# Attention with the values stationary: output by column, sums by a product with ones, reciprocals on ScalarE

## What is computed

```python
q = (xq @ Wq.T).reshape(B, SQ, NUM_HEADS, HEAD_DIM)      # B 8, SQ 256, 16 heads of 16
kv = (xkv @ Wkv.T).reshape(B, SKV, 2, NUM_HEADS, HEAD_DIM)  # SKV 77
att = jax.nn.softmax(jnp.einsum('bxhd,byhd->bhxy', q, k) * scale, axis=-1)
x = jnp.einsum('bhxy,byhd->bxhd', att, v).reshape(B, SQ, H)
return x @ Wout.T + bout
```

## Time and profile before

| | |
|---|---|
| median of 3 runs | 866.01 us (864.85 to 867.98) |
| profiled execution, its own time | 865.35 us |
| its span | 863.6 us, so 1.75 us lie outside of it |
| attention of layer 0, about | 6 to 145 us of the span |
| attention of layer 1, about | 242 to 381 us |

### The profile page before, as it was taken

How to read it: one execution, slowest core, us unless ns; L and a number is a source line. 1 busy time by engine, 2 the same in 40 slices (tenths; PEclk the granted TensorE clock), 3 DMA queues, 4 the chain that set the end, 5 groups by cost and what they waited for, 6 DMA issues and landing times.

```text
span 863.6 us, 17182 instructions
## 1 busy us (share of the span) xinstructions
PE 835.3 (97%) x5664; PEld 766.5 (89%) x5664; DVE 539.7 (62%) x1132; ACT 427.2 (49%) x938; POOL 276.7 (32%) x329
## 2 busy tenths in 40 slices
PE   8899999999979999999999999999999999999997
PEld 6788988999958989878887999999899999989986
DVE  4777764556687888465446574736456473645558
ACT  3666665777765666532323553616254361615331
POOL 5243414877773452145550001020200102020140
PEclk9999999999999999999999999999999999999999
DMA  5423237877520000201113432314233232413262
GB/s 209 116 69 128 66 117 286 260 219 224 175 77 8 7 6 6 87 17 44 60 44 90 133 90 70 106 41 134 60 97 95 80 89 61 128 39 100 64 194 99
DMA packets 74853, 86.26 MB, mean 100 GB/s; under 512 B 31418, under 2 KB 47484, under 8 KB 74678
## 3 DMA queue, kind: packets, MB, share of 16 engines
q1 hardware_dynamic: 67590, 69.65, 27.0%
q10 hardware_dynamic: 3664, 9.46, 3.1%
q0 software_dynamic: 3552, 6.55, 2.3%
HBM read 63.32 MB, written 23.63 MB: 101 GB/s over the span
## 4 chain that ended last, share of the span: by engine, by line
PE 83%; SPq 5%; DVE 4%; DMA 2%; ACT 2%; issue 2%; POOL 2%; DVEq 0%; ACTq 0%; POOLq 0%
PE score L292 13%; PE score L293 13%; PE score L294 13%; PE bank_p L298 11%; PE bank L603 7%; PE bank_p L299 6%; SPq L371 5%; PE bank_p L594 3%; PE bank L615 3%; PE bank L623 2%; PE bank L544 2%; PE score L583 2%; DMA v_blk<-values 1%; DVE residual L1911 1%; PE bank L957 1%
## 5 line engine op out<-in xcount | busy, mean ns | idle before, releaser
L1257 ACT ACTIVATE silu<-score 128x366 f32<-128x366 f32 (+1 forms) x144 | 72.6, 504 | 274.0 <-PE score L294 274.0
L298 PE MATMUL bank_p<-w_both,hid_hi 128*122 128x512 f32 (+1 forms) x432 | 152.5, 396 | 0.5 <-DVE hid_lo L1653 0.5
L1645 DVE TENSOR_TENSOR prod<-silu,score 128x366 f32<-128x366 f32 (+1 forms) x144 | 82.2, 571 | 110.6 <-ACT silu L1257 109.6
L292 PE MATMUL score<-xe_hi,w_both 128*128 128x366 f32 x448 | 147.4, 329 | 0.0
L293 PE MATMUL score<-xe_lo,w_both 128*128 128x366 f32 x448 | 147.3, 329 | 0.0
L294 PE MATMUL score<-xe_hi,w_both 128*128 128x366 f32 x448 | 147.2, 328 | 0.0
L2165 POOL DMA_INDIRECT slots_out<-yh,home_of x42 | 40.8, 972 | 331.0 <-DVE yh L1802 331.0
L299 PE MATMUL bank_p<-w_both,hid_lo 128*122 128x256 f32 (+1 forms) x432 | 120.8, 280 | 0.0
L298 PEld LDWEIGHTS bank_p<-w_both,hid_hi 128*122 128x122 f32 (+1 forms) x432 | 79.4, 184 | 21.5 <-DVE hid_lo L1653 1.6
L1981 POOL TENSOR_TENSOR w_both<-raw,w_both 128x512 fp32r<-128x512 f32 x62 | 83.4, 1374 | 24.6 <-ACT w_both L1037 17.8
L603 PE MATMUL bank<-v_blk,prob_t 128*128 128x136 f32 x640 | 83.9, 288 | 6.6 <-DMA v_blk<-values 6.2
(11 more groups left out here) (234 smaller groups left out, 1637.5 us busy)
## 6 DMA issues: line engine op xcount, KB each, us to landing
raw<-w_second_d SPq DMA_DIRECT2D x108, 256.0 KB, 2.7
raw<-w_first_d SPq DMA_DIRECT2D x56, 256.0 KB, 3.5
yh<-slot_rows SPq DMA_DIRECT2D x7, 674.6 KB
v_blk<-values SPq DMA_DIRECT2D x256, 5.0 KB, 2.0
slot_rows<-yh ACTq DMA_DIRECT2D x5, 771.0 KB, 3.3
slots_out<-yh ACTq DMA_DIRECT2D x5, 512.0 KB, 4.3
slot_rows<-yh SPq DMA_DIRECT2D x3, 771.0 KB, 5.7
raw<-w_first_d ACTq DMA_DIRECT2D x8, 256.0 KB, 3.8
```

The costliest lines, as they stand in the source:

```text
L292: nc.tensor.matmul(o, a_hi, b_hi, start=start, stop=False)
L298: nc.tensor.matmul(o, a_hi, b.rearrange("p c d -> p (c d)"), start=start, stop=False)
L1257: nc.scalar.activation(silu[0:rows_n, buf, 0:width], src, ACT.Silu).then_inc(silu_done, 1)
L1645: nc.vector.tensor_tensor(prod[0:rows_n, buf, 0:width], silu[0:rows_n, buf, 0:width], up, ALU.mult).then_inc(gu_free, 1)
```

## The change

- **Values stationary.** `weighted_values` now takes `v_main`, 64 keys of two heads by 32 columns, as the stationary operand, and `prob_t` of a head pair as the moving one, 256 tokens wide. Four such products write the four 32-partition parts of one PSUM bank; the other 13 keys of all pairs go through `v_rest`, one product of full width. So the output comes out by column, as `project_out` wants it, and `out_transposes` and `out_t`, with `o_q`, are gone. The sums come from the same moving operands against `ones_main` and `ones_rest`, into the second half of the bank, spread over each head's 16 rows.
- **Transposes.** `prob[u]` is laid out by head pair, 160 columns each. 128 of them are transposed as before (four transposes); the remaining 26 (padded to 32) of each pair go through four products with 32 columns of `prob` stationary and the identity moving, into four parts of `bank_p`.
- **Reciprocals.** ScalarE makes them as exp(-log(sum)) in `o_t` (`recip`), VectorE multiplies once (`normalise_out`). The table set that holds both functions is loaded by name.
- **Value bias.** It goes through the output projection once (`value_bias`, two products ahead of layer 1) and is added to the output's bias row.
- **Loads.** `v_main` and `v_rest` have two buffers each; a batch takes 12 DMAs instead of 16, all on one semaphore, and may start once the batch two before has been used. The zero padding of the values in DRAM is gone.
- **Order.** The products of both dt, the reciprocals, the projection and the router's logits change places in every step, and the first silu of the shared expert now stands behind the last reciprocal.

```diff
             def prob_transposes(g, u):
...
                 for grp, tiles in enumerate(((0, 1, 2), (3, 4))):
                     for i, j in enumerate(tiles):
-                        last = nc.tensor.transpose(bank_p[grp][:, i * P:(i + 1) * P], prob[u][:, j * P:(j + 1) * P], ident[:])
+                        if j < ROW_TILES:
+                            last = nc.tensor.transpose(bank_p[grp][:, i * P:(i + 1) * P], prob[u][:, j, 0:P], ident[:])
+                        else:
+                            for hg in range(ROW_TILES):
+                                last = nc.tensor.matmul(bank_p[grp][hg * PAIR:(hg + 1) * PAIR, i * P:(i + 1) * P], prob[u][:, hg, P:PW], ident[:],
+                                                        start=True, stop=True)
                     last.then_inc(pt_psum, 1)
 
-            def weighted_values(g, dt):
+            def weighted_values(g, par, dt, batches):
 
                 pe.wait_ge(pt_ready, 8 * g + 4 * dt + (6 if isinstance(g, int) and g == B and dt == 0 else 4))
-                pe.wait_ge(v_in[dt], 16 * HT * (g + 1))
-                for qt in range(HALVES):
-                    for j in range(PT):
-                        last = nc.tensor.matmul(bank[1][:, qt * VW:(qt + 1) * VW], prob_t[:, dt * PT + j, qt * P:(qt + 1) * P],
-                                                v_blk[:, dt * PT + j, :], start=j == 0, stop=j == PT - 1)
+                pe.wait_ge(v_in[par], 16 * V_LOADS * batches)
+                o, sums = bank[1][:, 0:S], bank[1][:, S:]
+                rest = prob_t[:, dt * PT + ROW_TILES, :]
+                nc.tensor.matmul(o, v_rest[:, par, dt, :], rest, start=True, stop=False)
+                nc.tensor.matmul(sums, ones_rest[:], rest, start=False, stop=False)
+                for hg in range(ROW_TILES):
+                    rows = slice(hg * PAIR, (hg + 1) * PAIR)
+                    nc.tensor.matmul(o[rows, :], v_main[:, par, dt * ROW_TILES + hg, :], prob_t[:, dt * PT + hg, :], start=False, stop=False)
+                for hg in range(ROW_TILES):
+                    rows = slice(hg * PAIR, (hg + 1) * PAIR)
+                    last = nc.tensor.matmul(sums[rows, :], ones_main[:], prob_t[:, dt * PT + hg, :], start=False, stop=True)
                 last.then_inc(pv_psum, 1)
 
-            def out_transposes(g):
-                pe.wait_ge(oq_ready, KT * g + KT)
-                transpose4(bank[0], o_q).then_inc(ot_psum, 1)
-
             def project_out(g, o):
-                pe.wait_ge(ot_ready, g + 1)
+                pe.wait_ge(ot_ready, KT * g + KT)
...
             def attention_step(layer, b, n, par, pair=None):
...
                 if some:
                     prob_transposes(g - 1, 2)
-                if two:
-                    out_transposes(g - 2)
-                if some:
-                    if layer == 0 and n == 1:
-                        pe.wait_ge(v_ready, 3)
-                    weighted_values(g - 1, 0)
-                if two:
-                    pe.wait_ge(ot_ready, g - 1)
                 if three:
                     norm2_t(g - 3)
+                if two:
+                    project_out(g - 2, bank[1])
                 if some:
                     prob_transposes(g - 1, 3)
...
+                if two:
+                    pe.wait_ge(x_new, g - 1)
                 if some:
-                    pe.wait_ge(oq_ready, KT * g - 1)
+                    weighted_values(g - 1, 1 - par, 0, batches)
+                if layer == 1 and three:
+                    pe.wait_ge(sub_done, 4 * g + 2)
+                    route_logits(g - 3, step_logits)
...
+                if some:
+                    pe.wait_ge(ot_ready, KT * g - 1)
+                    weighted_values(g - 1, 1 - par, 1, batches)
...
-            def out_t(layer, g):
...
+            def recip(g, dt):
+
+                act.wait_ge(pv_psum, KT * g + dt + 1)
+                nc.scalar.activation(o_t[:, dt, :], bank[1][:, S:], ACT.Ln).then_inc(ln_done, 1)
+                act.wait_ge(ln_done, KT * g + dt + 1)
+                nc.scalar.activation(o_t[:, dt, :], o_t[:, dt, :], ACT.Exp, scale=-1.0).then_inc(recip_done, 1)
...
             def normalise_out(g, dt):
 
-                dve.wait_ge(pv_psum, KT * g + dt + 1)
-                pv = bank[1][:, 0:HALVES * VW].rearrange("p (q c) -> p q c", q=HALVES)
-                nc.vector.reciprocal(recip[:], pv[:, :, P:]).then_inc(recip_done, 1)
                 dve.wait_ge(recip_done, KT * g + dt + 1)
-                nc.vector.tensor_tensor(o_q[:, :, dt * P:(dt + 1) * P].rearrange("p q (h d) -> p q h d", d=HD),
-                                        pv[:, :, 0:P].rearrange("p q (h d) -> p q h d", d=HD),
-                                        recip[:].unsqueeze(3).to_broadcast([P, HALVES, HT, HD]), ALU.mult).then_inc(oq_ready, 1)
+                nc.vector.tensor_tensor(o_t[:, dt, :], bank[1][:, 0:S], o_t[:, dt, :], ALU.mult).then_inc(ot_ready, 1)
...
-                if not isinstance(g, int) or g > 0:
-                    sp.wait_ge(pv_psum, KT * g - KT + 1 + dt)
...
+                if not isinstance(g, int) or g >= 2:
+                    sp.wait_ge(pv_psum, KT * g - KT)
...
+            def value_bias():
+
+                for dt in range(KT):
+                    last = nc.tensor.matmul(bank[0][:, 0:D], bias_cols[:, 1, 2, dt:dt + 1].to_broadcast([P, P]), wa[:, dt, O, :],
+                                            start=dt == 0, stop=dt == KT - 1)
+                last.then_inc(bv_psum, 1)
```

More of the change, by code:

```diff
@@ L633, in values, with placed, attention_step @@
                 last.then_inc(v_psum, 1)
-            def attention_step(layer, b, n, par):
+            def placed(layer, b):
+                return B // 2 * layer + b // 2 + 1
+            def attention_step(layer, b, n, par, pair=None):
                 g = b + B * layer
+                batches = placed(layer, b - 1) if pair is None else pair + B // 2 * layer + 2
                 start = layer == 0 and n == 0
@@ L691, in attention_step @@
                     queries(g + 1)
-                if final_step:
-                    pe.wait_ge(x_new, g - 1)
-                    if layer == 1:
-                        route_logits(g - 3, bank[1][:, HALVES * VW:])
-                    weighted_values(g - 1, 1)
                 prob_transposes(g, 1)
@@ L701, in attention_step @@
                     values(0, 2, bank[1])
-                if some and not final_step:
-                    if two:
-                        pe.wait_ge(x_new, g - 1)
-                    if layer == 1 and three:
-                        route_logits(g - 3, bank[1][:, HALVES * VW:])
-                    weighted_values(g - 1, 1)
-                if final_step:
-                    out_transposes(g - 1)
+                if some:
+                    pe.wait_ge(ot_ready, KT * g - 1)
+                    weighted_values(g - 1, 1 - par, 1, batches)
             def warm_array():
@@ L1116, in attention_step @@
                 final_step = n == B - 1
+                if two:
+                    recip(g - 2, 1)
                 if some:
                     probs_t(g - 1, 2)
-                if two:
-                    out_t(layer, g - 2)
-                if some:
-                    exps(g, 0)
                 if three:
@@ L1141, in attention_step @@
                     exps(g, 0)
-                if not two:
                     exps(g, 1)
+                if some:
+                    recip(g - 1, 0)
                 if layer == 1 and three:
@@ L1521, in attention_step @@
                 ahead = n is None or n < B - 2
+                if two:
+                    normalise_out(g - 2, 1)
                 if not (layer == 1 and n == 0):
                     max_sub(g, 0, start)
+                if start:
                     max_sub(g, 1, start)
-                if some:
-                    normalise_out(g - 1, 0)
-                if start:
                     scale_rows()
@@ L1532, in attention_step @@
                     add_attention(layer, b - 2, g - 2, bank[1])
+                if not start and not (layer == 1 and n == 0):
+                    max_sub(g, 1, start)
+                if two:
                     norm2_stats(b - 2, g - 2, layer == 0 and n == 2)
+                if layer == 1 and three:
+                    dve.wait_ge(s_psum, 4 * g + 4)
+                    keep_logits(b - 3, step_logits)
                 max_sub(g, 2, start)
-                if final_step:
-                    if layer == 1:
-                        dve.wait_ge(pv_psum, KT * g)
-                        keep_logits(b - 3, bank[1][:, HALVES * VW:])
-                    normalise_out(g - 1, 1)
+                if some:
+                    normalise_out(g - 1, 0)
                 max_sub(g, 3, start)
```

201 lines of the change are left out of this document (105 added, 96 removed).

## The result

The changed kernel takes 874.86 us (median of 5 runs, 871.37 to 875.49), the kernel before 866.01: 1.0089 times as long, with an interval of 1.0063 to 1.0115. The forecast was 869.0, within 852 to 888, with slower as the likeliest sign at 0.50. So the sign and the range held (the whole interval lies above 1, by less than 1.2%), and the middle was 6 us too low. The profiled execution took 875.43, 10.1 more than that of before; 3.7 were forecast. The next sections find the other 6.

What follows compares the result with a forecast made beforehand. TensorE's own work and waits were taken as the bound (busy 97% of the span). Terms 4.5 + 1.1 - 3.9 - 1.3 + 1.4 + 1.9 = +3.7 on 865.35 gave 869.0 us, range 852 to 888.

Steps and rivals of the forecast that it cites:

- Visits and sharing: TensorE's switches to column groups and back, 0.28 each, with four narrow products at once; +0.28 a batch, +4.5 over 16.
- The likeliest case: Column groups run four at once and each visit costs 0.28; 869.0 us, chance 0.62 together with rival 4.
- rivals 1 to 3: Column groups: 1, visits free, 857, chance 0.17; 2, overlap by one only, 924, 0.09; 3, no overlap, 994, 0.06.
- units: Each unit's transposes go from 0.54 to 0.93, four times +1.56; wider load before a two-record product adds 0.05 twice.
- the two values' products: In each batch, a values' product falls from 2.32 to 1.85, -0.47, twice -0.94.
- The wait for the residual's sum: A step's first values' product waits for VectorE's `add_attention` to free the projection's bank; 0.1 for 11 full steps, +1.1.
- ScalarE and VectorE in the steps: VectorE loses two reciprocals, ScalarE gains about +0.9 on 9.05 and 9.80; both stay below TensorE's step, costing nothing.
- rival 4: ScalarE's chain sets the step, residual wait 0.6 to 1 a step; 877, chance within the likeliest case's 0.62.
- Loads: -3.9: Two buffers and fewer issues remove layer 0's batch 5 hole, 2.13, and the slow product behind it, 4.09 instead of 2.32.
- the -1.3: Layer 0's start: the 2.73 wait for values goes, but twelve issues before batch 0 leave a wait of 1.4.
- Start of layer 1: Load wait stays; bias's product of four 0.218 records and a VectorE sum of some 0.5 are new; +1.4.
- Layer 1's tail: +1.9: Third shared piece waits 3.7 for last reciprocal, table load, silu and VectorE's product; covered waits of 1.5 and 0.3 offset it.

Runs made afterwards that it cites:

- the kernel with two subtractions: Changed kernel with the last 13 keys of all pairs in one full transpose, unstrided, the subtraction split into two instructions; 867.17 us, 1.0007.
- The new order: Changed kernel with second shared piece split around layer 1's last values' product, and last projection ahead of the third piece; 871.92 us, 1.0062.

## Why the prediction came out so

The terms of the sum by stage, beside both pairs of traces (the first pair is the one above, the second the two kernels once more):

| stage | forecast | first pair | second pair |
|---|---|---|---|
| layer 0, steps | -2.4 (8 x 0.28 + 0.6 - 5.2) | -2.8 | +0.2 |
| layer 0, tail | 0 | +2.7 | +2.0 |
| feed-forward, bias | +1.4 | +1.3 | +1.3 |
| layer 1, steps | +2.7 (8 x 0.28 + 0.5) | +2.5 | +2.5 |
| layer 1, tail | +1.9 | +6.0 | +4.6 |
| behind | 0 | +0.4 | +0.5 |
| sum | +3.6 | +10.0 | +11.0 |

The sums agree better than their parts do; two of the agreements are luck, and are called so below.

- **Visits and sharing: right.** The likeliest case (four at once, a visit that costs) is what the trace shows; rivals 1 to 3 fall, and the visit measured 0.25 for 0.28. A step of layer 0 takes 13.70 for 13.8 (before 13.46): units +1.4 for +1.66, the two values' products -0.7 for -0.94, output transposes -0.44. A full step of layer 1 takes 14.69, no more than before, since some 0.4 of short delays ahead of TensorE's groups, which I had not seen, went with the change (14.75 in the earlier trace rows, but 14.35 for the last full step, which has none).
- **Layer 1's steps: +2.5 for +2.7 is luck.** The five steps from the third batch's on, where 0.28 a batch and the residual's wait should have shown, take the same in both kernels, and in the second pair too (72.06 and 72.05). Before:

```profile
269.23:341.28 72.05, 71.63 (x629) 64.36 (x629) 60.82 (x144) 46.50 (x101) 30.50 (x42) 1.00 0.06 7
```

After, with one more window from the start of layer 1:

```profile
271.89:343.94 72.05, 72.05 (x752) 50.81 (x748) 57.91 (x135) 52.14 (x111) 30.42 (x42) 1.00 0.07 7
249.04:262.00 12.96, 11.44 (x76) 7.33 (x76) 9.85 (x18) 6.49 (x14) 8.60 (x11) 0.52 0.07 7
```

The +2.5 lies around them. The first two steps took 1.5 more in both pairs: in the first with the long stretch at half clock of the last row, in the second with the wait of 3.55 for values. And 1.0 is a product of the router that the new order puts ahead of the cut; it is missing from the tail, which so grew by 0.8 more than its +6.0 and +4.6 show.

- **The wait for the residual's sum: 0 instead of 1.1.** It was just hidden: the sum ends at 99.87, the product that needs it starts at 100.30. In the kernel with two subtractions it shows, 0.5 a time.
- **ScalarE and VectorE in the steps: right.** ScalarE is busy for 10.48 and 10.90 of a step (+1.4 and +1.1 for +0.9), still far from setting it; rival 4 did not come.
- **Loads: -3.9 was too much.** The wait of 2 at batch 5 is gone; the slow clock behind it, 1.8 of the 3.9, was in one of two traces. Layer 0's first wait is 1.26 for the 1.4 forecast, but nothing of the -1.3 is left by the sixth group of scores (47.48 for 47.11 before, 47.34 for 46.65 in the second pair). Other waits for values have come (0 in one trace, 4.5 in the other). That layer 0's steps hit -2.8 for -2.4 is luck as well: the second pair has +0.2.
- **Start of layer 1: +1.3 in the feed-forward's stage for +1.4**, of which the bias product is 0.68 (for 0.87). The rest was not traced to VectorE's sum.
- **Layer 0's tail: the step that is missing, +2.7 and +2.0.** I costed what TensorE does in the steps and let the last step pass as one more. Its ScalarE queue has 4.1 us of load issues, and the product that covered them was moved away. Moving the loads gives 2.9 to 3.4 back, slow clock included.
- **Layer 1's tail: +1.9 forecast, +6.0 and +4.6 in the two pairs of traces.** The mechanism was right to the tenth (3.7 idle, 3.67 measured). The size was off because I priced the idle time and not the clock behind it, though the earlier trace rows shows just that: 2.4 us in the third piece in both traces, and 1.6 in a second stretch in one. The new order takes all of it away. With the router's product counted in, some 1 us of the tail's growth is left that idle time and clock do not explain; it was not followed.

## What to carry to other kernels

Four products side by side in column groups cost as much as one full one, but each visit costs 0.25 us, so many small visits (64 of them here) lose more than the narrow shape saves; laying the leftovers out next to each other, so that they make one full product, was worth 8 us. When work is moved between queues, read the written-out first and last steps as separate cases: the long DMA issues and table loads stand there, and what covered them may have moved. An idle stretch of 2 to 4 us on a busy TensorE is to be priced with the slow products that may follow it (behind 2.58 and 3.67 in both traces, behind 1.97 in one of two). And a sum that comes out right says little until each of its terms is held against a stretch of the trace.

## What the hardware showed unexpectedly

- VectorE's subtraction of 616 columns takes 799 ns with pieces of neighbouring columns written, 1314 when each column is written four apart. TensorE reads a stationary with that stride at little loss (four transposes 0.47 instead of 0.44, and 0.59 instead of 0.49 right behind the scores).
- Two subtractions of 512 and 104 columns take 692 and 256 ns by their own records, 0.95 together, but from start to the start of what follows the pair takes 0.78 and the one 0.72 (103.97 to 104.69 in the changed kernel): instructions of one engine overlap at their ends, and a split cost 0.06.
- Issuing two loads took ScalarE 1.43 us in the changed kernel, and 3.16 where SyncE issued large transfers at the same time; nothing else was varied to show that this is the cause.
